# A four-layer cross-attention kernel: L1's query weights treated behind their product, twelve unread products at the front, and a new order of steps

## The reference, cut to what matters

```
L0: x = x + softmax((x Wq + bq)(ctx Wk + bk)^T / 16)(ctx Wv + bv) Wo + bo
L1: text = x; for (keys, a) in ((ctx, "a"), (side, "v")):
      out_a = attention(LN(text; g1, b1) Wq + bq, LN(keys; g2, b2) Wk + bk, ... Wv + bv) Wo + bo
    s = out_a + out_v + text;   x = LN(s; ln_g, ln_b) fc_W + fc_b + s
L2: softmax over the queries of (x Wq + bq)(ctx Wk + bk)^T / 16, times (ctx Wv + bv); x = LN(. + x; gamma, beta)
L3: like L0, with its own weights
```

## Time and profile before

| | |
|---|---|
| median of 3 runs | 600.8 us (600.71 to 601.79) |
| profiled execution, own time | 600.17 us |
| its span, first to last instruction | 598.1 us |
| granted TensorE clock, mean | 0.985 of full |
| PE busy | 574.3 us (96%) |
| POOL / DVE / ACT busy | 502.4 (84%) / 470.1 (79%) / 444.9 (74%) |
| HBM read / written | 35.14 MB / 8.39 MB |
| chain that ended last | PE 87%, DVE 6%, issue 2%, ACT 1%, DMA 1%, SP queue 1% |

### The profile page before, as it was taken

The page is one execution under the profiler, slowest core; times in us unless marked ns, Lnnn a source line. Parts: engine busy times, 40 slices in busy tenths (PEclk is TensorE's granted clock), DMA queues, the critical chain, the costliest instruction groups (busy, mean ns, idle before and its releaser), DMA issues.

```text
span 598.1 us, 16329 instructions
## 1 busy us (share of the span) xinstructions
PE 574.3 (96%) x4712; PEld 559.4 (94%) x4712; DVE 470.1 (79%) x1470; ACT 444.9 (74%) x1520; POOL 502.4 (84%) x700
## 2 busy tenths in 40 slices
PE   4699999999999999999999999999999999999994
PEld 3699999999999999999999999999999999999973
DVE  3997698887888787788888788888877785887972
ACT  2268977777887877878976968788778898677552
POOL 4589998999899997989898598999999895776671
PEclk9799999999999999999999999999999999999997
DMA  8961211122222220222222122222121100000011
GB/s 241 359 219 45 90 45 47 47 63 80 90 72 71 81 76 33 81 81 73 63 79 68 42 81 81 71 87 76 63 81 63 38 9 19 19 3 19 19 54 54
DMA packets 30375, 44.58 MB, mean 75 GB/s; under 512 B 2768, under 2 KB 22096, under 8 KB 30288
## 3 DMA queue, kind: packets, MB, share of 16 engines
q1 hardware_dynamic: 30288, 43.54, 22.2%
HBM read 35.14 MB, written 8.39 MB: 73 GB/s over the span
## 4 chain that ended last, share of the span: by engine, by line
PE 87%; DVE 6%; issue 2%; ACT 1%; DMA 1%; SPq 1%; POOL 0%; DVEq 0%; ACTq 0%; POOLq 0%
PE bank L672 14%; PE bank L685 9%; PE bank L655 9%; PE bank L679 9%; PE bank L663 7%; PE bank L696 5%; PE bank L823 5%; PE bank L698 5%; PE bank L697 5%; PE bank L801 5%; PE bank L713 4%; PE bank L785 3%; PE bank L786 3%; PE bank L787 3%; PE bank L814 1%
## 5 line engine op out<-in xcount | busy, mean ns | idle before, releaser
L915 ACT ACTIVATE prob_L<-bank,neg_max_L 128x128 f32<-128x128 f32 x320 | 114.4, 378 | 18.5 <-DVE neg_max_L L1241 18.3
L1396 POOL TENSOR_TENSOR rstd_ln<-var_eps_ln,minus_half 128x2 f32<-128x2 f32 x64 | 45.1, 705 | 29.6 <-ACT var_eps_ln L925 29.3
L915 ACT ACTIVATION_READ_ACCUMULATOR prob_L<-bank,neg_max_L 128x1 f32 x320 | 69.4, 217 | 0.0
L1241 DVE TENSOR_REDUCE neg_max_L<-bank 128x2 f32<-128x256 f32 (+1 forms) x128 | 59.1, 476 | 11.7 <-PE bank L679 9.4
L1055 DVE TENSOR_TENSOR oT_lo_L<-bank,oT_hi_L 128x256 fp32r<-128x256 f32 (+1 forms) x96 | 48.2, 504 | 21.3 <-ACT oT_hi_L L868 20.3
L868 ACT ACTIVATE xT_hi_L<-bank 128x512 fp32r<-128x512 f32 (+1 forms) x96 | 58.4, 612 | 8.1 <-PE bank L655 5.8
L868 ACT ACTIVATE oT_hi_L<-bank 128x256 fp32r<-128x256 f32 (+1 forms) x96 | 44.9, 472 | 20.7 <-PE bank L685 19.2
L868 ACT ACTIVATE probT_L<-bank 128x256 f32<-128x256 f32 (+1 forms) x96 | 45.4, 473 | 9.0 <-PE bank L663 8.8
L1204 DVE BATCH_NORM_STATS2 stats_ln<-x 128x6 f32<-128x256 f32 x128 | 47.7, 414 | 0.9
L1055 DVE TENSOR_TENSOR xT_lo_L<-bank,xT_hi_L 128x512 fp32r<-128x512 f32 x64 | 43.6, 681 | 6.0 <-ACT xT_hi_L L868 5.3
L663 PE MATMUL bank<-ident,prob_L 128*128 128x128 f32 x256 | 43.7, 274 | 2.1 <-ACT prob_L L915 2.1
(11 more groups left out here) (225 smaller groups left out, 2351.4 us busy)
## 6 DMA issues: line engine op xcount, KB each, us to landing
x_in<-in_x SPq DMA_DIRECT2D x32, 512.0 KB, 3.5
ctx_in<-in_ctx SPq DMA_DIRECT2D x32, 256.0 KB, 3.2
out<-y SPq DMA_DIRECT2D x32, 256.0 KB, 2.2
side_in<-in_side SPq DMA_DIRECT2D x32, 128.0 KB, 2.0
WqT_L<-in_L_WqT SPq DMA_DIRECT2D x3, 256.0 KB, 4.9
Wo_L<-in_L_Wo SPq DMA_DIRECT2D x2, 256.0 KB, 5.7
WkT_L<-in_L_WkT SPq DMA_DIRECT2D x3, 128.0 KB, 5.4
WvT_L<-in_L_WvT SPq DMA_DIRECT2D x2, 128.0 KB, 5.3
```

The costliest lines, as they stand in the source:

```text
L915: last = activation(at(prob[k], g)[:, b, :], block(bank, b), ACT.Exp, bias=at(neg_max[k], g)[:, b:b + 1], accum_out=at(total[k], g)[:, b:b ...
L1241: dve.tensor_reduce(at(neg_max[k], g)[:], scores, AX.X, ALU.max, negate=True).then_inc(done[f"max_{k}"], 1)
L1396: pool.tensor_tensor(at(rstd[k], g)[:], at(var_eps[k], g)[:], minus_half[:, 0:n], ALU.pow).then_inc(done[f"rstd_{k}"], 1)
```

## The change

1. `wq_a` on VectorE goes, for both attentions of L1. The product `M_a` is taken from the untouched WqT. Behind it ScalarE makes `M0_a` (a plain copy) and `M1_a` (times the column g1), TensorE takes the mean over the rows by a product with a constant matrix (`mean_M_a`, two products), VectorE subtracts it (`M_centred_a`), ScalarE rounds it (`M_hi_a`), and GpSimd makes the remainder (`M_lo_a`). `m_L1a` and `m_L1v` have two more products each, `M0` with b1. The four row loads of g1 and b1 (128 KB each) go; g1 and b1 now come with `cols`, which is 34 columns wide and not 26.
2. The subtraction of the mean from WkT and WvT moves from VectorE to ScalarE (eight instructions of 128 x 128); `F_lo`, `Wv2_lo`, `M_lo_L1a`, `M_lo_L1v` move from VectorE to GpSimd.
3. TensorE starts with `run_up`: twelve float32 products of the constant matrix with itself into the last bank, which nobody reads. GpSimd writes that constant first (`first_constant`).
4. Both tables are new. Loads, preparations and all steps of the 32 groups stand in another order. The number of copies of each buffer is unchanged.

```diff
-PREPARATIONS = {"M_L0": 395, "N_L0": 528, "m_L0": 484, "n_L0": 615, "M_L1a": 1381, "N_L1a": 1614, "m_L1a": 1470, "M_L1v": 2081, "N_L1v":
+PREPARATIONS = {"run_up": 300, "M_L2": 833, "k_L2": 1051, "n_fc": 2758, "mean_fc": 2889, "N_L1a": 4312, "n_L0": 1834, "N_L0": 1611, "M_L0":
...
             def product_M(a):
                     if a in LN_KEYS:
-                        prepared(pe, f"wq_{a}")
                         prepared(pe, f"wk_{a}")
...
-                    terms = [(stage[a]["WkT"][:, h, :], bqp[a][:, h, :] if a in LN_KEYS else col(f"{a}_bq", h, scaled_cols)) for h in range(T)]
-                    if a == "L3":
+                    terms = [(stage[a]["WkT"][:, h, :], col(f"{a}_bq", h, scaled_cols)) for h in range(T)]
+                    if a != "L0":
+                        prepared(pe, f"M0_{a}")
+                        terms += [(M0[a][:, t, :], col(f"{a}_b1", t, scaled_cols)) for t in range(T)]
...
+            def mean_M(a):
+                    prepared(pe, "first_constant")
+                    prepared(pe, f"M1_{a}")
+                    bank = bank_for(pe, f"mean_M_{a}")
+                    for t in range(T):
+                        last = mm(bank[:, 0:P], mean_of_D[:], M1[a][:, t, :], start=t == 0, stop=t == T - 1)
...
+            def run_up():
+                prepared(pe, "first_constant")
+                for n in range(RUN_UP):
+                    mm(banks[-1][:, 0:P], mean_of_D[:], mean_of_D[:], start=True, stop=True)
...
+            def M1_of(a):
+                    for t in range(T):
+                        last = activation(M1[a][:, t, :], block(bank_of(f"M_{a}"), t), ACT.Copy, scale=col(f"{a}_g1", t, scaled_cols))
...
-            def wq_of(a):
-                    dve.tensor_tensor(product_of[:], w[:], rows[f"{a}_b1"][:].unsqueeze(1).to_broadcast([P, T, D]), ALU.mult).then_inc(done["small"], 1)
-                    dve.tensor_reduce(b1[:], product_of[:], AX.X, ALU.add).then_inc(done["small"], 1)
-                    dve.tensor_tensor(b1[:], b1[:], cols[:, COLS.index(f"{a}_bq"), :], ALU.add).then_inc(done["small"], 1)
-                    dve.tensor_scalar(bqp[a][:].rearrange("p t o -> p (t o)"), b1[:], SCALE, None, ALU.mult)
-                    dve.tensor_tensor(w[:], w[:], rows[f"{a}_g1"][:].unsqueeze(1).to_broadcast([P, T, D]), ALU.mult).then_inc(done["small"], 1)
-                    centred(w, sums[f"wq_{a}"], before + 4)
...
+            def M_centred(a):
+                    prepared(dve, f"mean_M_{a}")
+                    dve.tensor_tensor(M1[a][:], M1[a][:], mean.unsqueeze(1).to_broadcast([P, T, P]), ALU.subtract)
...
+            def M_lo_of(a):
+                    prepared(pool, f"M_hi_{a}")
+                    pool.tensor_tensor(flat(M_lo[a]), flat(M1[a]), flat(M_hi[a]).bitcast(F32), ALU.subtract)
```

More of the change, by code:

```diff
@@ L858, in tensor_program @@
                      {f"M_{a}": product_M(a) for a in ATTENTIONS} | {f"N_{a}": product_N(a) for a in ATTENTIONS}
-                     | {f"m_{a}": query_bias(a) for a in ATTENTIONS}
+                     | {f"m_{a}": query_bias(a) for a in ATTENTIONS} | {f"mean_M_{a}": mean_M(a) for a in LN_KEYS}
                      | {f"n_{k}": output_bias(k, LAYERS[k]) for k in LAYERS}
-                     | {"n_fc": n_fc, "mean_fc": mean_fc, "M_L2": M_L2, "k_L2": k_L2})
+                     | {"run_up": run_up, "n_fc": n_fc, "mean_fc": mean_fc, "M_L2": M_L2, "k_L2": k_L2})
         def scalar_program(act):
@@ L871, in M0_L3, with centred, of, M0_of @@
                 prepared(act, "M_L3")
-                copied(flat(M0), bank_of("M_L3")[:, 0:D], "M0_L3")
+                copied(flat(M0["L3"]), bank_of("M_L3")[:, 0:D], "M0_L3")
+            def centred(step, w, less_mean, summed):
+                def of():
+                    prepared(act, summed)
+                    for t in range(T):
+                        last = activation(w[:, t, :], w[:, t, :], ACT.Identity, bias=less_mean[:, t:t + 1])
+                    last.then_inc(done[step], 1)
+                return of
+            def M0_of(a):
+                def of():
+                    prepared(act, f"M_{a}")
+                    copied(flat(M0[a]), bank_of(f"M_{a}")[:, 0:D], f"M0_{a}")
+                return of
+            def M1_of(a):
+                def of():
+                    prepared(act, f"M_{a}")
+                    prepared(act, "scaled")
+                    for t in range(T):
+                        last = activation(M1[a][:, t, :], block(bank_of(f"M_{a}"), t), ACT.Copy, scale=col(f"{a}_g1", t, scaled_cols))
+                    last.then_inc(done[f"M1_{a}"], 1)
+                return of
             def M_hi_of(a):
                 def of():
+                    if a in LN_KEYS:
+                        prepared(act, f"M_centred_{a}")
+                        copied(flat(M_hi[a]), flat(M1[a]), f"M_hi_{a}")
+                        return
                     prepared(act, f"M_{a}")
@@ L1063, in scaled_less @@
                 return dve.scalar_tensor_tensor(out=to, in0=of, scalar=scale, in1=hi.bitcast(F32), op0=ALU.mult, op1=ALU.subtract)
-            def centred(w, sums_of, wait):
-                n = w.shape[2]
-                dve.tensor_reduce(sums_of[:], w[:], AX.X, ALU.add, negate=True).then_inc(done["small"], 1)
-                dve.wait_ge(done["small"], wait + 1)
-                dve.tensor_scalar(sums_of[:], sums_of[:], 1.0 / n, None, ALU.mult).then_inc(done["small"], 1)
-                dve.wait_ge(done["small"], wait + 2)
-                for t in range(T):
-                    last = dve.tensor_scalar(w[:, t, :], w[:, t, :], sums_of[:, t:t + 1], None, ALU.add)
-                return last
             small = {}
@@ L1100, in wq_of @@
+                    prepared(dve, gained)
+                    before = smalls(1)
+                    dve.tensor_reduce(sums_of[:], w[:], AX.X, ALU.add, negate=True).then_inc(done["small"], 1)
+                    dve.wait_ge(done["small"], before + 1)
+                    dve.tensor_scalar(sums_of[:], sums_of[:], 1.0 / P, None, ALU.mult).then_inc(done[step], 1)
                 return of
-            def wk_of(a):
+            def M_centred(a):
                 def of():
-                    prepared(dve, f"wk_gained_{a}")
-                    before = smalls(2)
-                    centred(stage[a]["WkT"], sums[f"wk_{a}"], before).then_inc(done[f"wk_{a}"], 1)
-                return of
@@ L1121, in of @@
                     b2 = sums[f"b2_{a}"]
-                    dve.tensor_reduce(b2[:], product["wv"][:], AX.X, ALU.add).then_inc(done["small"], 1)
+                    dve.tensor_reduce(b2[:], product_wv[:], AX.X, ALU.add).then_inc(done["small"], 1)
                     dve.wait_ge(done["small"], before + 1)
@@ L1375, in of @@
                     w = stage[a]["WvT"]
-                    pool.tensor_tensor(product["wv"][:], w[:], rows[f"{a}_b2"][:].unsqueeze(1).to_broadcast([P, T, P]), ALU.mult).then_inc(done["zeroed"], 1)
+                    pool.tensor_tensor(product_wv[:], w[:], rows[f"{a}_b2"][:].unsqueeze(1).to_broadcast([P, T, P]), ALU.mult).then_inc(done["zeroed"], 1)
                     pool.wait_ge(done["zeroed"], 2 if a == "L1a" else 3)
```

157 lines of the change are left out of this document (77 added, 80 removed), and 344 rows, old and new, of tables (PREPARATIONS, STARTS).

## The result

The changed kernel takes 591.05 us in the median of 4 runs (589.79 to 592.21), the kernel before beside it 600.87 (600.71 to 601.79, 4 runs). The ratio is 0.9833, with an interval of 0.9808 to 0.9858: 9.8 us faster, where 8.1 were forecast (600.8 to 592.7). The profiled execution took 591.77 us with a span of 590.0, against 600.17 and 598.1 before; so the profiles must explain 8.1 us of span.

The account below looks back on a forecast made before the run. TensorE, busy 574.3 of 598.1 us, was taken as the bound, with time lost in waits and slow clock. Terms -7.0 + 1.7 - 3.0 + 0.4 = -7.9 from 600.17 give 592.3, plus 0.4 is 592.7; range 588.5 to 597.5.

Parts of the forecast that it names:

- a clock of 0.50 between 8 and 20 us: In the opening: listed beforehand as a sign that the forecast was wrong and the clock had stayed at half.
- the opening: Up to the second group's Q_L0: lost time falls from 18.0 to 11.0 us, gaining 7.0 (4.9 to 8.2).
- the end: Last group's chain: other work fills TensorE's gaps, gaining 3.0 us, bounds 0 to 4.
- the middle: All 32 groups in new order: a few missed hand-overs lose 0.4 us, bounds 0 and 4.
- GpSimd sets this point: Second group's Q_L0: GpSimd's x_bias steps and lo_L0 end at 24.8 us, TensorE's work at 24.0; Q_L0 starts at 25.0.
- I count the new opening at full clock from 7 us on: Opening: the account prices TensorE's work from 7 us at full clock, with no slow stretch.
- rival 1: Opening: gaps keep the clock at half, costing about 3.8 us, giving 596.5; chance 0.13.
- The added work: TensorE: mean_M for both attentions and two further columns in each m cost 1.7 us at full clock.
- The rival of one hand-over wait a group: Closer packed groups: TensorE waits 0.56 us in 28 groups, 15.7 us, giving 608; slower case, chance 0.07.
- The removed loads: Load queue: four 128 KB loads fewer save 2.0 us of issue, already counted inside the landings.
- Rival 3: Opening loads land earlier, Wo_L0 by 13.1 us, and the end gives 4 us: 590.5; chance 0.15.
- rival 2: GpSimd bounds the opening up to 60 us and its added 3.5 us show in full: 596.2; chance 0.09.

Follow-up runs that it names:

- e10: The kernel of e4 timed once more, on another comparison beside the unchanged changed kernel: 590.74 us, ratio 0.9819.
- e11: The kernel of e4 with GpSimd's second and third x_bias moved behind lo_L0 of the second group: 590.57 us, ratio 0.9817.
- e4: The changed kernel with thirteen more unread products in TensorE's gaps of the opening: 590.35 us, ratio 0.9819.
- e7: The kernel of e2 with twenty unread products: six at the front, seven before the first Q_L0, seven before M_L1a: 599.36 us, ratio 0.9975.
- e2: The changed kernel with the old tables and no run-up, keeping the new weight treatment and the moves to ScalarE and GpSimd: 603.48 us, ratio 1.0041.
- e3: The changed kernel with the last group's L3 steps moved later, so only group 30's OUT stands beside the last chain: 594.3 us, ratio 0.9888.
- e5: The kernel before with only the constant filled first and the twelve unread products at the front added: 602.29 us, ratio 1.0014.
- e6: The changed kernel with new tables and run-up kept, but the old weight treatment and row loads (points 1 and 2) restored: 610.32 us, ratio 1.0147.

## Why the prediction was right, point by point

The sign, the size and the places were right: 592.7 forecast with 588.5 to 597.5, 591.05 measured. That the sum is so close is partly luck: the opening gave 1.1 us less than forecast, the end 0.6 more and the middle 0.9 more, and these cancel. One of its own signs of being wrong did come: a clock of 0.50 between 8 and 20 us. By its own terms:

- **The opening, 7.0 forecast, 5.9 in the profile.** T_keys at 8.45 (8.5 forecast), N_L0 at 15.97 (16.0), the second Q_L0 at 26.06 (25.0). Two steps of the account failed, though their times nearly hold. N_L0 was to wait for Wo_L0; that load was issued at 9.93 us and took 4.9, so it was in at 14.8, and N_L0 stood behind S_L0, which began late and ran at half clock. That the 16.0 came out is luck; where the clock doesn't fall, in e10, N_L0 starts at 15.27 us. And "GpSimd sets this point" is refuted: M_L3, on TensorE itself, ends where the second Q_L0 begins, and e11 makes GpSimd 2.4 us earlier there and gains nothing. The sum behind it was wrong too: the nine blocks that the prediction lists for TensorE add up to 6.45 us at its own prices, not 5.8, so TensorE is done at 24.65 and not at 24.0, against 24.8 for GpSimd. That is a near tie, and so it was in the profile, 26.1 against 25.7.
- **"I count the new opening at full clock from 7 us on" failed,** which is rival 1 in part, given 0.13. In the profile the clock was at half from 14.5 to 17.9 us, and the 2.9 us of work from 15 on at half speed cost about 1.4. The rival's place and cause were right (the gap around 12 to 14 us), its 3.8 us too much for the median. The gap came from what the prediction named as a doubt: ctx 1 landed at 11.36 and its steps stood ahead of M_hi_L0 and M_lo_L0. The Trainium skill ("TensorE: Matmul & The Clock Gate", What's actually happening) has the clock released by activity and fallen back without it. The windows of e4 against the changed kernel's agree: no wait from 10 to 20 us, no fall. e7 and e2 agree only in part: with the products in the waits the clock was back at 16.6 us, but in e2 it stayed low for 9.4 us of nearly steady work (last section).
- **The added work, 1.7.** TensorE's busy sum rises by 2.0 us in spite of less time at half clock, with the 4.5 of the run-up in it; the term was not measured alone.
- **The end, 3.0 forecast.** 2.3 of less idle and 1.3 of the last products at full clock, 3.6 in the profile; 2.5 to 3.2 by the medians of e3 and about 4 by its profile. The second of these the prediction didn't name: it read the last rows of before for their gaps and not for their clock. The page shows it, whose clock row ends in a 7 and not, as said further up, in a 9:

```profile
PEclk9799999999999999999999999999999999999997
```

- **The middle, 0.4 lost with bounds 0 and 4.** 0.5 gained. The rival of one hand-over wait a group (608 us) did not come.
- **The removed loads.** Taken as inside the landings; not tried alone. Rival 3's early landing didn't come: Wo_L0 took 4.9 us. What the prediction takes there from the Trainium skill ("DMA: Bandwidth & Descriptors", Anatomy of one DMA) is stated for transfers that GpSimd issues; SyncE issues all of these loads, so it says little about them.
- **GpSimd's 3.5 us (rival 2) did not show.** GpSimd is busy 3.2 us more, and e11 shows 2.4 us of room on it at the point where it was to bind.

What the prediction did not see at all is that its terms don't add. It priced the treatment, the run-up and the order as parts of one account, and that held for all of them together. Apart, the treatment, the run-up, and the order with the run-up each lose (e2, e5, e6); only the end's fill stands by itself (e3). The order without both the others wasn't tried.

## What to carry to other kernels

Where TensorE is the bound, a wait in the opening can cost its own length and then half of the time that the clock stays low behind it: some 2.1 us behind the 6.6 us wait before (4.3 at half), 1.4 behind two waits of 2.1 us together in the changed kernel, 4.1 in e2 by e7. So cost it as both, read the clock column of the windows behind each wait (and the lengths of like products where it has not yet fallen once), and consider unread products in it. To tell an opening from the rest, measure both sides of one fixed point, here the second Q_L0: an edit of the end then can't be mistaken for luck in the opening. A change made of a cheaper treatment and an order that needs it should be priced and tried as a whole: the treatment without the order, or the order without the treatment, can show the wrong sign, as they did here. Where two engines reach a point within a microsecond of each other in the account, say that either may set it; shortening one alone gave nothing here (e11).
